# A decoder layer on one core: the second FFN product turned round, W_down stationary and the activations moving in 512 columns

## The chip, the core and the metric

The kernel runs on one core of one Trainium2 chip. The time is device microseconds of one execution; a result is the median of several executions. The kernel before takes 132.09 us (three runs, 131.9 to 132.27).

## What is computed

A pre-norm decoder layer for 16 sequences of 64 tokens with 256 features (1024 tokens, float32), in three steps with a residual each. The reference, cut to what matters here:

```python
x = x + self_attention(layernorm(x))            # 16 heads, causal, ALiBi, biases
x = x + cross_readout(layernorm(x), ctx, mask)  # scores with ctx, softmax, readout of ctx
def ffn(inputs, up_kernel, up_bias, down_kernel, down_bias):
    q_up, s_up = quantize_to_mxfp4(up_kernel, 32)
    x = mxfp4_matmul(inputs, q_up, s_up, 32) + up_bias        # 256 -> 1024
    x = gelu(x)
    q_dn, s_dn = quantize_to_mxfp4(down_kernel, 32)
    return mxfp4_matmul(x, q_dn, s_dn, 32) + down_bias        # 1024 -> 256
x = x + ffn(layernorm(x), ...)
```

The weights of the FFN are quantised in the kernel, in blocks of 32 rows with a power of two as scale. The quantised values are exact in bfloat16 and in float32r.

## The kernel before

The 1024 tokens are eight tiles of 128 (`TILES`). Two halves of four tiles go through the first layer norm and the projections q, k and v; from there the self attention, the cross attention and the third layer norm run tile by tile. The FFN runs in four groups of two tiles (`GT`, 256 tokens) and, in each, over eight blocks of 128 hidden features (`FC`). A step i = 8g + f of it has five stages:

- `up` (TensorE, L1160): four matmuls of 256 columns in float16 with `w_up_q` stationary, two parts of the normalised activations, into bank 0 or 1 in turn.
- `gelu` (ScalarE, L778): bias and gelu from the bank to `h_sb`.
- `round` (GpSimd, L630): `h_hi`, the value rounded to float32r.
- `split` (VectorE, L982): `h_lo`, what the rounding left.
- `down` (TensorE, L1176): for both tiles and both parts one matmul of 256 columns. The activations (`h_hi`, `h_lo`, 128 hidden features by 128 tokens) are stationary, the weights `w_down_q` move. All 32 matmuls of a group add up in one bank, tokens on the partitions.

After the last step of a group `final` (VectorE, L989) adds the bank to `x_sb`, once for each tile, and `store` (SyncE, L581) writes the tile of 128 KB. The bias of the second product has been added to `x_sb` before, by `add_down` on GpSimd (L634), once for each tile after its third layer norm, as `add_bo` (L591) adds the bias of the output projection.

The layer norms: `stats` on VectorE (L810, L811), `rstd` on GpSimd (L599, L603, L607), `norm` on ScalarE (L660) or VectorE (L819), `turn` on TensorE (L1015, transposes), `turn_copy` on ScalarE (L669, L672). Other stages that the prediction names: the projections q and k (L1028, float32 matmuls of 512 columns), the cross attention's scores (L1110, two float32 matmuls of 128 columns, and L1112), its transpose of the probabilities (L1118), readout (L1123).

The order of the work is not written by hand. `stages()` lists every stage with its engine, a duration, what it waits for and its banks; `schedule()` walks this table as a list scheduler and returns one order, and every engine's program goes through that order and emits its own stages. Among the ready stages that could start within `PATIENCE` of the first, the one with the longest way to the end wins, and `URGENCY` and `DRIFT` add to this way by name. The durations only set the order; on the chip the engines wait for each other by semaphores, and each engine's queue is in order:

```python
limit = starts[first] + patience.get(engine, 0.06)
key = max((k for k in starts if table[k][0] == engine and starts[k] <= limit), key=lambda k: (way[k], k))
```

A bank is claimed before it is written: TensorE waits in `claim` until the reader of what was last in the bank is done.

## Time and profile before

| what | value |
|---|---|
| median of 3 runs | 132.09 us (131.9 to 132.27) |
| the profiled execution, its own time | 132.44 us |
| its span in the trace | 130.6 us |
| TensorE busy (PE) | 116.4 us, 89% |
| TensorE weight loads (PEld) | 87.8 us, 67% |
| VectorE busy (DVE) | 103.5 us, 79% |
| ScalarE busy (ACT) | 88.7 us, 68% |
| GpSimd busy (POOL) | 81.5 us, 62% |
| data moved | 10.69 MB, mean 82 GB/s |

The page is one execution, taken by the hardware profiler. The span runs from the first to the last instruction or transfer that it shows; the execution's own time is 1.8 us longer. Busy time counts an instruction from its start to its end, and matmuls overlap: where two matmuls of a queue start 0.12 us apart, each may last 0.28 us. So distances between starts tell what TensorE can do, and durations do not. A float32 matmul stands in the trace as two matmuls (two passes), a float32 transpose, a float16 and a float32r matmul as one.

### The profile page before, as it was taken

The page shows a single profiled execution, that of the slowest core. Times are in us where ns is not written, and L with a number is a line of the kernel's source. Part 1 is how long each engine was busy: PE and PEld are TensorE (multiplying, and loading weights), DVE is VectorE, ACT ScalarE, POOL GpSimd, SP SyncE. Part 2 cuts the span into 40 slices and gives each one's busy share as a digit, 9 for nine tenths or more (in the row PEclk, how much of TensorE's full clock was granted, in tenths as well). Part 3 has the DMA queues.
Part 4 walks back from the last instruction along what each step waited for, and adds up shares of the span by engine and source line. Part 5 has one row for each costly group of instructions (what it writes and reads, how often), then busy time and mean ns, then how long its engine had stood idle before and what let it go on. Part 6 is the DMA issues. An engine that isn't in the chain of part 4 may idle for free.

```text
span 130.6 us, 3224 instructions
## 1 busy us (share of the span) xinstructions
PE 116.4 (89%) x1072; PEld 87.8 (67%) x1072; DVE 103.5 (79%) x227; ACT 88.7 (68%) x190; POOL 81.5 (62%) x144
## 2 busy tenths in 40 slices
PE   0997999698999899999989996979989599999990
PEld 0996447265534786677767684758878389999980
DVE  5678794799999999899999998778743985685632
ACT  1224679776999987977757875687957877754520
POOL 7685700153999976638038898787764567894330
PEclk9999999999999999999999999999999999999999
DMA  4799906999500000000000000000000200020202
GB/s 119 206 364 374 354 16 260 365 356 373 119 3 3 0 5 0 5 0 0 5 0 0 0 8 0 0 0 3 5 0 0 79 1 5 0 80 0 85 3 80
DMA packets 8879, 10.69 MB, mean 82 GB/s; under 512 B 1664, under 2 KB 7936, under 8 KB 8736
## 3 DMA queue, kind: packets, MB, share of 16 engines
q1 hardware_dynamic: 7776, 9.64, 22.1%
q10 hardware_dynamic: 1088, 0.86, 2.0%
q8 instruction: 9, 0.15, 0.5%
q14 instruction: 6, 0.05, 0.1%
HBM read 9.45 MB, written 1.05 MB: 80 GB/s over the span
## 4 chain that ended last, share of the span: by engine, by line
PE 29%; DVE 26%; POOL 18%; issue 18%; ACT 6%; DVEq 1%; POOLq 0%; ACTq 0%
POOL h_hi L630 6%; PE bank L1028 5%; PE bank L1176 5%; PE bank L1160 5%; DVE s_sb L857 5%; POOL rstd L603 5%; DVE s_max L862 4%; POOL var_eps L599 3%; PE bank L1040 3%; POOL x_sb L634 2%; DVE stats L810 2%; PE bank L1067 2%; PE bank L1059 2%; PE bank L1015 2%; POOL s_sb L641 2%
## 5 line engine op out<-in xcount | busy, mean ns | idle before, releaser
L641 POOL TENSOR_TENSOR s_sb<-s_sb,s_max 128x512 f32<-128x512 f32 x16 | 18.6, 1165 | 18.4 <-DVE s_max L862 18.2
L982 DVE TENSOR_TENSOR h_lo<-h_sb,h_hi 128x256 fp32r<-128x256 f32 x32 | 15.1, 485 | 7.6 <-POOL h_hi L630 7.5
L1160 PE MATMUL bank<-xn_T,w_up_q 128*128 128x256 f16 x128 | 19.4, 274 | 1.4 <-ACT h_sb L778 1.4
L778 ACT ACTIVATE h_sb<-bank,bias_cols 128x256 f32<-128x256 f32 x32 | 15.0, 472 | 7.7 <-PE bank L1160 5.9
L1176 PE MATMUL bank<-w_down_q,h_hi 128*128 128x256 f32 x64 | 19.2, 324 | 0.2 <-DVE h_lo L982 0.2
L630 POOL CAST h_hi<-h_sb 128x256 fp32r<-128x256 f32 x32 | 13.9, 440 | 8.0 <-ACT h_sb L778 7.6
L660 ACT ACTIVATE xn<-x_sb,shift,rstd 128x256 f32<-128x256 f32 x20 | 12.0, 599 | 7.7 <-POOL shift L607 3.2
L1176 PE MATMUL bank<-w_down_q,h_lo 128*128 128x256 f32 x64 | 16.4, 280 | 0.0
L603 POOL TENSOR_TENSOR rstd<-var_eps,minus_half 128x1 f32<-128x1 f32 x24 | 14.9, 622 | 2.0
L1028 PE MATMUL bank<-xn_T,w_T 128*128 128x512 f32 x32 | 14.7, 601 | 0.8 <-ACT xn_T L672 0.8
L599 POOL TENSOR_SCALAR var_eps<-mean_var 128x1 f32<-128x1 f32 x24 | 7.3, 304 | 10.7 <-DVE mean_var L811 9.5
L1160 PEld LDWEIGHTS bank<-xn_T,w_up_q 128*128 128x128 bf16 x128 | 10.5, 97 | 4.2 <-issue 1.4
L1176 PEld LDWEIGHTS bank<-w_down_q,h_hi 128*128 128x128 f32 x64 | 12.1, 189 | 0.8 <-issue 0.4
L1176 PEld LDWEIGHTS bank<-w_down_q,h_lo 128*128 128x128 f32 x64 | 12.2, 190 | 0.1
L1081 PEld LDWEIGHTS bank<-v,p_T 128*64 128x64 f32 x256 | 8.8, 137 | 4.5 <-issue 4.5
L857 DVE TENSOR_TENSOR s_sb<-bank,alibi_sb 128x512 f32<-128x512 f32 x16 | 10.9, 684 | 0.9 <-PE bank L1059 0.9
L724 ACT ACTIVATE p_T<-bank 128x512 f32<-128x512 f32 x16 | 9.5, 594 | 3.0 <-PE bank L1067 2.1
L1015 PE MATMUL bank<-const,xn 128*128 128x128 f32 x48 | 10.0, 296 | 1.6 <-ACT xn L660 1.2
L862 DVE TENSOR_REDUCE s_max<-s_sb 128x8 f32<-128x512 f32 x16 | 10.8, 675 | 0.1
L591 POOL TENSOR_TENSOR x_sb<-x_sb,row_biases_all 128x256 f32<-128x256 f32 x8 | 10.7, 1364 | 0.0
L1028 PEld LDWEIGHTS bank<-xn_T,w_T 128*128 128x128 f32 x32 | 5.8, 190 | 7.1 <-issue 7.1
L1081 PE MATMUL bank<-v,p_T 128*64 128x34 f32 x256 | 10.5, 226 | 0.0
(89 smaller groups left out, 265.5 us busy)
## 6 DMA issues: line engine op xcount, KB each, us to landing
raw_T<-in_W_up_T_dram SPq DMA_DIRECT2D x1, 1024.0 KB, 9.2
raw<-in_W_up_dram SPq DMA_DIRECT2D x1, 1024.0 KB, 11.5
raw_T<-in_W_down_T_dram SPq DMA_DIRECT2D x1, 1024.0 KB, 5.0
raw<-in_W_down_dram SPq DMA_DIRECT2D x1, 1024.0 KB, 7.8
ctx_T<-in_ctx_by_feature_dram SPq DMA_DIRECT2D x1, 1024.0 KB, 10.1
ctx_sb<-in_ctx_dram SPq DMA_DIRECT2D x1, 1024.0 KB, 13.8
out_dram<-x_sb SPq DMA_DIRECT2D x8, 128.0 KB, 1.7
x_sb<-in_x_dram SPq DMA_DIRECT2D x4, 128.0 KB, 3.1
```

The lines of the kernel that those rows point to most:

```text
L603: pool.tensor_tensor(rstd[:, n, t:t + 1], var_eps[:, n, t:t + 1], minus_half[:, :], ALU.pow).then_inc(rstd_ready[n], 1)
L630: pool.tensor_copy(h_hi[:, i % H_RING, :], h_sb[:, i % GELU_RING, :]).then_inc(rounded, 1)
L641: pool.tensor_tensor(tile, tile, s_max[:, u % S_RING, :].unsqueeze(2).broadcast_to([P, HC, S]), ALU.subtract).then_inc(centred, 1)
L778: act.activation(h_sb[:, i % GELU_RING, :], bank[up_bank(i)][:, 0:GN], ACT.Gelu_apprx_tanh, bias=bias_cols[:, BUP + f:BUP + f + 1], scale= ...
L857: dve.tensor_tensor(s_sb[:, u % S_RING, :], bank[u % EC][:, :], alibi_sb[:, u % EC, :], ALU.add).then_inc(scores_added, 1)
L862: dve.tensor_reduce(s_max[:, u % S_RING, :], s_sb[:, u % S_RING, :].rearrange("p (h k) -> p h k", h=HC), AX_X, ALU.max).then_inc(max_ready, 1)
L982: dve.tensor_tensor(h_lo[:, i % H_RING, :], h_sb[:, i % GELU_RING, :], h_hi[:, i % H_RING, :].bitcast(F32), ALU.subtract).then_inc(split_r ...
L1015: last = pe.transpose(dst[:, c * P:(c + 1) * P], xn[:, ring[t % len(ring)], c * P:(c + 1) * P], ident)
L1028: last = pe.matmul(dst[:, :], w_T[:, m, i, c * P:(c + 1) * P], half_tokens(h, i), start=(i == 0), stop=(i == EC - 1))
L1081: last = pe.matmul(dst[b * S:(b + 1) * S, first:first + width], p_T[:, u % 2, g, b * S:(b + 1) * S], v2[:, 2 * t + b, c * 4 + g, :, :].rea ...
L1160: last = pe.matmul(dst[:, 0:GN], w_up_q[:, c, f * P:(f + 1) * P], xn_T16[:, g * GT:(g + 1) * GT, at16:at16 + P], start=(k == 0), stop=(k = ...
L1176: last = pe.matmul(dst, src[:, i % H_RING, t * P:(t + 1) * P], w_down_q[:, f, :], start=(f == 0 and part == 0 and t == 0), stop=(f == FC - ...
```

## The change

The second product is turned round. `h_hi` and `h_lo` become the two halves of one tile `h_parts`, so that 512 columns (256 tokens in two parts) move at once, and `w_down_q` is stationary. A `down` stage is then two matmuls, one for each half of the 256 output features, each into a bank of its own, so a group holds two banks (`DOWN_BANKS`). The bank holds features by tokens: the sum of the high part in columns 0 to 255, that of the low part in columns 256 to 511.

What `final` did in token order no longer fits, so:

- `residual` (TensorE, new, eight stages): for each tile two matmuls with x stationary and the identity moving, 128 columns each, which add x, turned, into the bank's high half.
- `low_sum` (ScalarE, new, eight stages): the low half with the bias by feature goes to `x_sb`, whose two tiles of the group are free then.
- `final` (VectorE, eight stages as before): the high half is added to that. `store` writes 128 features by 256 tokens, 128 KB, to an output laid out by features.
- `add_down` on GpSimd is gone, and the load of the two row biases becomes a load of one.

The durations of many stages in `stages()` are renewed, `URGENCY`, `DRIFT` and `PATIENCE` are replaced, and with them the order on every engine. The diff, cut to its core:

```diff
-        add("add_down", (t,), "pool", 0.7, [("norm", (LN3, t))])
...
-            add("down", (i,), "pe", 0.56, [("split", (i,)), ("q_out", (DOWN, 1))], banks, ("final", (tiles[-1],)))
+            add("down", (i,), "pe", 0.39, [("split", (i,)), ("q_out", (DOWN, 1))], banks, [("final", (g, c)) for c in range(EC)])
         for t in tiles:
-            add("final", (t,), "dve", 0.33, [("down", (FC * g + FC - 1,)), ("add_down", (t,))])
-            add("store", (t,), "sp", 1.0, [("final", (t,))])
+            add("residual", (t,), "pe", 0.24, [("x2", (t,)), ("down", (FC * g,))])
+        for c in range(EC):
+            add("low_sum", (g, c), "act", 0.4, [("down", (FC * g + FC - 1,))] + [("residual", (t,)) for t in tiles])
+            add("final", (g, c), "dve", 0.35, [("low_sum", (g, c))])
+            add("store", (g, c), "sp", 1.0, [("final", (g, c))])
...
-        for name, us in (("q_divide", 1.13), ("q_exponent", 0.6), ("q_step", 0.6), ("q_add", 1.13), ("q_round", 1.13),
+        for name, us in (("q_divide", 1.85), ("q_exponent", 0.6), ("q_step", 0.6), ("q_add", 1.13), ("q_round", 1.13),
...
 PATIENCE = {
-    "pool": 0.54, "act": 0.04, "dve": 0.0, "pe": 0.0,
+    "pool": 0.34, "dve": 0.18, "act": 0.14, "pe": 0.1,
 }
...
-        h_hi = sb("h_hi", [P, H_RING, GN], F32R)
-        h_lo = sb("h_lo", [P, H_RING, GN], F32R)
+        h_parts = sb("h_parts", [P, H_RING, 2, GN], F32R)
+        h_hi, h_lo = h_parts[:, :, 0, :], h_parts[:, :, 1, :]
...
+                if stage == "low_sum":
+                    g, c = at
+                    act.wait_ge(down_ready, FC * (g + 1))
+                    act.wait_ge(residual_turned, GT * (g + 1))
+                    act.activation(out_by_feature(g, c), bank[down_bank(g, c)][:, GN:2 * GN], ACT.Identity,
+                                   bias=bias_cols[:, B_DOWN + c:B_DOWN + c + 1]).then_inc(low_sum_ready, 1)
...
                 if stage == "final":
-                    t, = at
-                    g = t // GT
-                    dve.wait_ge(down_ready, FC * (g + 1))
-                    dve.wait_ge(b_down_added, t + 1)
-                    dve.tensor_tensor(x_sb[:, t, :], bank[down_bank(g)][:, (t % GT) * E:(t % GT + 1) * E],
-                                      x_sb[:, t, :], ALU.add).then_inc(final_ready, 1)
+                    g, c = at
+                    dve.wait_ge(low_sum_ready, EC * g + c + 1)
+                    dve.tensor_tensor(out_by_feature(g, c), bank[down_bank(g, c)][:, 0:GN], out_by_feature(g, c),
+                                      ALU.add).then_inc(final_ready, 1)
...
-                    if f == 0:
-                        claim(down_bank(g), (final_ready, GT * (g + 1)))
-                    for t in range(GT):
-                        dst = bank[down_bank(g)][:, t * E:(t + 1) * E]
-                        for part, src in enumerate((h_hi, h_lo)):
-
-                            last = pe.matmul(dst, src[:, i % H_RING, t * P:(t + 1) * P], w_down_q[:, f, :],
-                                             start=(f == 0 and part == 0 and t == 0),
-                                             stop=(f == FC - 1 and part == 1), skip_group_check=True)
+                    for c in range(EC):
+                        if f == 0:
+                            claim(down_bank(g, c), (final_ready, EC * g + c + 1))
+                        last = pe.matmul(bank[down_bank(g, c)][:, :], w_down_q[:, f, c * P:(c + 1) * P],
+                                         h_parts[:, i % H_RING, :, :].rearrange("p s n -> p (s n)"),
+                                         start=(f == 0), stop=(f == FC - 1), skip_group_check=True)
                     last.then_inc(down_ready, 1)
+                if stage == "residual":
+                    t, = at
+                    g = t // GT
+                    pe.wait_ge(x2_ready, t + 1)
+                    first = t % GT * P
+                    for c in range(EC):
+                        last = pe.matmul(bank[down_bank(g, c)][:, first:first + P], x_sb[:, t, c * P:(c + 1) * P],
+                                         ident, start=False, stop=False, skip_group_check=True)
+                    last.then_inc(residual_turned, 1)
...
-DOWN_BANKS = (2, 3, 2, 3)
+DOWN_BANKS = ((2, 3), (4, 2), (3, 4), (5, 7))
```

How the order moves, at three places. The rows are instructions of one engine in program order, output before the arrow, operands behind it; numbers at names are banks.

TensorE, the end of the program. Before, the last up stage (into bank 1) is followed by four down stages and nothing else; the first of them and the beginning of the next:

```order
L1160 MATMUL bank1<-xn_T,w_up_q 128x256 x4
L1176 MATMUL bank3<-w_down_q,h_hi 128x256
L1176 MATMUL bank3<-w_down_q,h_lo 128x256
L1176 MATMUL bank3<-w_down_q,h_hi 128x256
L1176 MATMUL bank3<-w_down_q,h_lo 128x256
```

With the change, from the same up stage on, to the last matmul:

```order
L1166 MATMUL bank1<-xn_T,w_up_q 128x256 x4
L1179 MATMUL bank5<-h_parts,w_down_q 128x512
L1179 MATMUL bank7<-h_parts,w_down_q 128x512
L1189 MATMUL bank5<-const,x_sb 128x128
L1189 MATMUL bank7<-const,x_sb 128x128
L1179 MATMUL bank5<-h_parts,w_down_q 128x512
L1179 MATMUL bank7<-h_parts,w_down_q 128x512
L1189 MATMUL bank5<-const,x_sb 128x128
L1189 MATMUL bank7<-const,x_sb 128x128
L1179 MATMUL bank5<-h_parts,w_down_q 128x512
L1179 MATMUL bank7<-h_parts,w_down_q 128x512
```

The residuals of tiles 6 and 7 now stand between the last four down stages (L1179), of which the fourth ends the program.

TensorE, the end of the second group with the change (its banks are 4 and 2). L1129 is the cross attention's readout of the last tile, L1166 the up stages of steps 19, 20 and 21:

```order
L1129 MATMUL bank5<-ctx_sb,xp_T 128x256
L1179 MATMUL bank4<-h_parts,w_down_q 128x512
L1179 MATMUL bank2<-h_parts,w_down_q 128x512
L1179 MATMUL bank4<-h_parts,w_down_q 128x512
L1179 MATMUL bank2<-h_parts,w_down_q 128x512
L1166 MATMUL bank1<-xn_T,w_up_q 128x256 x4
L1166 MATMUL bank0<-xn_T,w_up_q 128x256 x4
L1166 MATMUL bank1<-xn_T,w_up_q 128x256 x4
L1179 MATMUL bank3<-h_parts,w_down_q 128x512
L1179 MATMUL bank4<-h_parts,w_down_q 128x512
```

Before, up and down stages take turns here, step by step. Now the eight down stages of the group stand with one up stage among them, and three up stages follow the last.

ScalarE, the same place with the change. L779 is gelu, L786 `low_sum`, L740 the exponential of the cross attention, L749 the copy of its probabilities:

```order
L740 ACT_TABLE_LOAD
L740 ACTIVATE xs_sb,xs_sum<-bank7,xs_negmax 128x128
L749 ACTIVATE xp_T<-bank6,valid 128x128
L740 ACTIVATE xs_sb,xs_sum<-bank7,xs_negmax 128x128
L749 ACTIVATE xp_T<-bank6,valid 128x128
L779 ACT_TABLE_LOAD
L779 ACTIVATE h_sb<-bank1,bias_cols 128x256
L786 ACTIVATE x_sb<-bank4,bias_cols 128x256
L779 ACTIVATE h_sb<-bank0,bias_cols 128x256
L786 ACTIVATE x_sb<-bank2,bias_cols 128x256
L779 ACTIVATE h_sb<-bank1,bias_cols 128x256
L661 ACTIVATE xn<-x_sb,shift,rstd 128x256
```

Before, ScalarE's gelus (L778) there have only normalisations and copies of the layer norm between them:

```order
L778 ACTIVATE h_sb<-bank0,bias_cols 128x256
L669 ACTIVATE xn_T<-bank6 128x256
L778 ACTIVATE h_sb<-bank1,bias_cols 128x256
```

So the gelu that frees bank 0 now stands behind the first copy, which waits for the last down stage of the group.

## Rows read from the trace of the kernel before

**Rows 1.** The page's section 1: busy us, share of the span, instructions.
```profile
PE 116.4 (89%) x1072; PEld 87.8 (67%) x1072; DVE 103.5 (79%) x227; ACT 88.7 (68%) x190; POOL 81.5 (62%) x144
```

**Rows 2.** Busy time in stretches: from:to, length, each engine's us and count, granted clock.
```profile
30.00:80.00 50.00, 48.41 (x528) 33.97 (x527) 48.31 (x93) 41.01 (x88) 36.32 (x45) 1.00 0.10 29
80.00:90.00 10.00, 7.78 (x80) 5.98 (x78) 7.72 (x18) 7.19 (x17) 7.90 (x13) 1.00 0.00 1
...
104.00:117.00 13.00, 12.63 (x107) 11.46 (x108) 9.59 (x23) 9.00 (x22) 10.53 (x24) 1.00 0.10 32
117.00:126.00 9.00, 9.00 (x80) 8.29 (x80) 5.22 (x13) 4.68 (x10) 4.28 (x11) 1.00 0.10 32
```

**Rows 3.** Timeline of TensorE: start us, us, what [idle before <-releaser].
```profile
81.68 0.44 PE L1015 MATMUL bank<-const,xn 128*128 128x128 f32 x2 [1.23 <-ACT xn L660]
...
103.66 0.30 PE L1118 MATMUL bank<-const,xs_sb 128*128 128x128 f32 x1 [0.92 <-DVE xn_T L825]
104.36 0.60 PE L1160 MATMUL bank<-xn_T,w_up_q 128*128 128x256 f16 x4 [0.40 <-ACT h_sb L778]
```

**Rows 4.** TensorE: one steady step in the timeline; source views of up and down.
```profile
110.39 0.61 PE L1160 MATMUL bank<-xn_T,w_up_q 128*128 128x256 f16 x4
110.75 0.37 PE L1176 MATMUL bank<-w_down_q,h_hi 128*128 128x256 f32 x1
110.96 0.28 PE L1176 MATMUL bank<-w_down_q,h_lo 128*128 128x256 f32 x1
...
111.19 0.28 PE L1176 MATMUL bank<-w_down_q,h_lo 128*128 128x256 f32 x1
111.32 0.61 PE L1160 MATMUL bank<-xn_T,w_up_q 128*128 128x256 f16 x4
...
L1160 PE MATMUL bank<-xn_T,w_up_q x36: 272/273/283, 117.2 to 124.9; 128*128 128x256 f16 x36
...
L1176 PE MATMUL bank<-w_down_q,h_hi x64: 278/287/470, 89.6 to 127.1; 128*128 128x256 f32 x64
```

**Rows 5.** Timeline of the weight loads of the same down stage.
```profile
110.84 0.19 PEld L1176 LDWEIGHTS bank<-w_down_q,h_lo 128*128 128x128 f32 x1
110.96 0.19 PEld L1176 LDWEIGHTS bank<-w_down_q,h_hi 128*128 128x128 f32 x1
```

**Rows 6.** Chain that ended last: the projections q and k, start us, us.
```profile
12.85 7.10 PE bank L1028 x16
```

**Rows 7.** Timeline of TensorE: a pair of transposes, the cross attention's scores.
```profile
98.57 0.38 PE L1015 MATMUL bank<-const,xn 128*128 128x128 f32 x2
99.81 0.62 PE L1110 MATMUL bank<-ctx_T,xn_T 128*128 128x128 f32 x4
```

**Rows 8.** Timeline of all engines at the end of the program.
```profile
124.60 0.61 PE L1160 MATMUL bank<-xn_T,w_up_q 128*128 128x256 f16 x4
126.83 0.35 PE L1176 MATMUL bank<-w_down_q,h_hi 128*128 128x256 f32 x1 [0.20 <-DVE h_lo L982]
127.27 0.28 PE L1176 MATMUL bank<-w_down_q,h_lo 128*128 128x256 f32 x1
127.58 0.76 DVE L989 TENSOR_TENSOR x_sb<-bank,x_sb 128x256 f32<-128x256 f32 x2 [0.90 <-PE bank L1176]
```

**Rows 9.** GpSimd's bias additions: their group, and pieces of the chain.
```profile
L634 POOL TENSOR_TENSOR x_sb<-x_sb,row_biases_all 128x256 f32<-128x256 f32 x8 | 5.8, 726 | 2.8 <-ACT xn L660 2.8
...
78.26 0.68 POOL x_sb L634
84.31 0.72 POOL x_sb L634
113.09 0.68 POOL x_sb L634
```

**Rows 10.** ScalarE: a copy of 256 columns from a bank; a gelu.
```profile
L672 ACT ACTIVATE xn_T<-bank 128x256 f32<-128x256 f32 x16 | 6.0, 378 | 4.6 <-PE bank L1015 4.6
...
104.37 0.47 ACT L778 ACTIVATE h_sb<-bank,bias_cols 128x256 f32<-128x256 f32 x1
```

107 lines of the change are left out of this document (52 added, 55 removed).

## The prediction

> **What bounds the kernel now.** I read the page's busy line first: TensorE is busy for 116.4 of 130.6 us, VectorE for 103.5, ScalarE for 88.7, GpSimd for 81.5 [rows 1]. That is an average, so the table by stretches comes next [rows 2]. From 30 to 80 us TensorE and VectorE are both about 97% busy. From 80 to 90 us TensorE falls to 7.78 of 10 us. From 104 us on it is busy almost without a break, and from 117 to 126 us for 9.00 of 9.00 us, at a granted clock of 1.00, its 2.4 GHz level, while VectorE needs 5.22 and ScalarE 4.68 us of the nine. So in the last quarter, where the change lies, TensorE's own work is the time, and a saved microsecond there is a saved microsecond. Third, TensorE's waits: after the start there are few, and the long ones lie between 80 and 105 us: 1.23 us for a normalised tile from ScalarE, 0.92 and 0.40 us around one of ScalarE's table loads [rows 3].
>
> **The down matmuls.** In the steady stretch one step is four up matmuls and four down matmuls, each of 256 columns. The up stages of two neighbouring steps start at 110.39 and 111.32 [rows 4]; over eight steps the source view gives 117.2 to 124.9 for first and last up matmul, less the 0.34 us by which the fourth starts after the first, so (7.7 - 0.34) / 8 = 0.92 us. Eight matmuls share it: 0.115 us each. At 2.4 GHz 256 columns take 0.107 us, if a column takes a cycle, which the up matmuls bear out: four in 0.61 us, less the 0.27 us of the last one, are 0.112 us apart. The change streams the same 2048 columns in six matmuls instead of eight. What can be gained is therefore only what lies between 0.117 us (the distance of the down matmuls) and 0.107 us, per matmul saved. No row shows a one-pass matmul of float32r with 512 columns. The bounds: 0.235 us, twice the present one, so no gain; and 0.213 us, columns alone. The nearest row is the float32 matmul of 512 columns, which the trace shows as two passes; 16 of them take 7.10 us [rows 6], 0.444 us each for 1024 cycles, so 0.222 us for 512. I take that: a down stage falls from 4 x 0.117 = 0.468 to 0.444 us, and 32 of them give back **0.8 us** (bounds 0 and 1.3).
>
> The 64 weight loads that go lie beside the matmuls: a load lasts 190 ns, yet the loads start 0.12 us apart, as the matmuls do [rows 4, 5]. So I count nothing more for them.
> The Trainium skill's page TensorE: Matmul & The Clock Gate (Back-to-back issue gap) gives a warm matmul N / 2.4 GHz plus 2.5 ns; by that rule, as an estimate, a down stage would save 2 x 2.5 ns and the whole change 0.2 us in place of the 0.8. The measured distance of the down matmuls, 0.117 us, is larger than the rule's 0.109, so the trace goes with the larger saving.
>
> **The residual by TensorE.** New are eight stages of two float32 matmuls with 128 columns, 16 matmuls in all, which turn x and add it into the bank. They are plain matmuls, not transposes. The cross attention's scores are that form: four passes for two matmuls, in 0.62 us less the last one's 0.28, so 0.113 us apart [rows 7]. With a little for the change of form around them, two matmuls cost 4 x 0.115 = 0.46 us, eight stages **3.7 us**. Below, a pair of transposes (0.38 us less 0.28, so about 0.1 us apart, one pass each) would make it 0.22 us a stage, 1.8 us in all. The nearest row is the scores', same type and same columns, so 3.7 us stand. On the path: tiles 2 to 5 wholly, 1.84 us; tiles 0 and 1 come while TensorE still has waits, I count half, 0.46 us; tiles 6 and 7 stand between the last down stages. There the old kernel has a hole: the last up stage starts at 124.60, its fourth matmul at 124.94, and the last down stage only at 126.83 because it waits for gelu, rounding and split [rows 8]. Between are three down stages, 1.40 us, so some 0.5 us are free (1.89 - 1.40, hardly less with the shorter stages), and of the 0.92 us 0.4 remain. Sum on the path **+2.7 us**.
>
> **The end.** Now two VectorE additions of 0.41 us follow the last matmul, from 127.58 to 128.34 [rows 8]. Afterwards ScalarE first evacuates the lower half with the bias. The row for such a copy is 378 ns [rows 10]; add a handover of 0.05 us, which the step from 127.55 to 127.58 and others bound. The second addition waits for the second copy, which starts some 0.3 us after the first: first copy to 0.41, first addition to 0.84, second to 1.25 us, against 0.76 now: **+0.5 us**. The stores are eight of 128 KB before and after.
>
> **GpSimd.** Eight additions of 726 ns leave, 5.8 us. Most ran where GpSimd had room. On the chain of waits pieces of them stand at 78.26 and 84.31, 0.68 and 0.72 us, just where TensorE is short of work and ScalarE waits for GpSimd's statistics; those at 113.09 and later lie under a full TensorE [rows 9]. **-1.4 us**; bounds 0 (the cover is VectorE, late next in that stretch) and -2.1.
>
> **ScalarE.** It gets eight copies, 3.0 us, in a stretch where it is about half busy, so no price for the time they take. But its queue is in order. Behind the first copy of the second group stands the gelu that frees bank 0 for the second of three up stages; both wait for the last down stage of the group. After that stage ends: 0.16 us until its result is there (0.28 less 0.117 [rows 8]), 0.05, copy 0.3 to 0.38, gelu 0.47 [rows 10], 0.05; about 1.05 us, of which the one up stage that can run covers 0.45. The next up stage stands behind another copy and gelu, 0.75 us, less 0.45. Together **+1.1 us** with a remainder for the normalisation between the next gelus. In the first and third group an up stage and another down stage cover the copy, and I count nothing. Against it, the new order fills the two holes of 0.92 and 0.40 us [rows 3] with a row of down stages, **-1.3 us**.
>
> Renewed durations and urgencies move many stages before 80 us too; there both big engines are full [rows 2], and none of their work goes, so nothing is counted. The bias load only becomes smaller. At the start GpSimd clears the mask before its first statistics instead of between them, the same work in another place; nothing.
>
> **Sum:** -0.8 + 2.7 + 0.5 - 1.4 + 1.1 - 1.3 = +0.8 us. The profiled execution took 132.44 us with a span of 130.6; its own would become 133.2. It stood 0.35 us above the median of three, 132.09, so I forecast 132.9 us. A measurement can tell about 0.3% from no change, 0.4 us, so "same" is 131.7 to 132.5.
>
> **The rivals.**
> *Cheap residual (faster).* The identity streams like in a transpose, 0.22 us a stage: on the path 0.46 x 2 for tiles 2 to 5, 0.23 for 0 and 1, nothing for 6 and 7, so 1.15 in place of 2.7; and the wide matmul takes 0.217 us, a saving of 1.1. The sum is then -1.05: 131.0 us, and 129.9 us if the hold on ScalarE does not come either. For it: TensorE's waits between 80 and 90 us are large. Against it: the scores' rows. Chance 0.30.
> *Weight loads were not hidden (faster).* If all that the steady step has above its columns, 0.92 - 0.853 = 0.07 us, came from four exposed loads and left with the change, 32 steps would give 2.2 us in place of 0.8: 131.5 us. Rows 5 speak against it: the loads overlap each other. Chance 0.05.
> The page named above (The mechanism, under packing) says that a weight load overlaps running matmuls only in other row groups, which all these loads share; by its load time of 128 / 1.2 GHz, 107 ns, an estimate would be 6.8 us less for 64 loads. The trace disagrees: eight loads and 2048 columns together take 0.92 us.
> *It cancels out (same).* Residuals fill waits to the last, or GpSimd's relief is worth 2.1 us: 132.1 us. Chance 0.15.
> *ScalarE is held in every group (slower still).* If in the first and third group too the copy reaches the head of the queue before the last down stage is done, two more holds of 1.1 us: 135.1 us; one of them gives 134.0. It decides from the point where the gelu ahead of the copy ends before that down stage. Chance 0.11.
> *The wide matmul is no cheaper (slower).* 0.235 us each, so the change does not do what it says: 133.7 us. Chance 0.05.
>
> **Numbers.** Forecast, slower by about 0.8 us, own range 132.5 to 134.3: 0.34. Slower in all 0.34 + 0.11 + 0.05 = 0.50, faster 0.35, same 0.15. The range from 129.9 to 135.0 us leaves out part of the cheap residual and the far end of the holds.
>
> **What would show it.** Down matmuls 0.22 us apart, steady step 0.89 to 0.90 us. Residual matmuls in passes 0.11 to 0.12 us apart, four to a stage. After the last matmul 1.25 us to the end of the last addition. One wait of TensorE for ScalarE of half a microsecond or more behind the eighth down stage of the second group. GpSimd's busy time 5.8 us less. The forecast is wrong if a residual stage takes 0.25 us, if the wide matmuls come less than 0.213 us apart, or if the time before the first down stage, now at 89.6 us [rows 4], changes by more than the work moved across it.

## The result, and the profile after

| | before | changed |
|---|---|---|
| median | 132.18 us (131.9 to 132.86, 4 runs) | **135.56 us** (134.79 to 136.28, 4 runs) |
| the profiled execution, its span | 132.44 us, 130.6 us | 136.28 us, 133.9 us |

The changed kernel is slower: ratio 1.026, 95% interval 1.021 to 1.031, that is 3.4 us in place of the 0.8 us forecast, and above the range (up to 135.0 us). The profiled execution stands 0.7 us above its median. Executions over 1.5% above the fastest of the same kernel are left out of its median and ratio; that touches one execution of the kernel before and one kernel below, whose trace is of such an execution.

The busy line of the page, and its chain by engine (before, the chain had 29% on TensorE):

```profile
PE 119.8 (89%) x1040; PEld 84.8 (63%) x1040; DVE 102.0 (76%) x227; ACT 90.6 (68%) x198; POOL 73.8 (55%) x136
...
PE 72%; ACT 8%; DVE 7%; issue 6%; POOL 2%; DMA 2%; ACTq 0%; DVEq 0%
```

The stretches, to be read against [rows 2]:

```profile
30.00:80.00 50.00, 49.03 (x518) 33.82 (x519) 47.96 (x94) 42.54 (x93) 34.67 (x46) 1.00 0.14 46
80.00:90.00 10.00, 7.82 (x83) 5.97 (x84) 8.42 (x24) 6.05 (x19) 4.75 (x9) 1.00 0.00 1
...
104.00:117.00 13.00, 12.30 (x75) 8.86 (x74) 8.21 (x23) 9.90 (x22) 5.93 (x16) 1.00 0.12 42
117.00:126.00 9.00, 9.00 (x60) 6.46 (x60) 5.31 (x14) 5.17 (x12) 3.67 (x8) 1.00 0.05 18
```

TensorE is busy 3.4 us longer and waits about as much as before. From 80 to 90 us GpSimd's work fell from 7.90 to 4.75 us, yet TensorE is no fuller than it was (7.82 against 7.78). From 104 to 117 us ScalarE is fuller than before, 9.90 us against 9.00. The granted clock is 1.00 in all of these.

Timeline of TensorE in the steady stretch and at the end of the program, and the two other engines behind it:

```profile
120.27 0.60 PE L1166 MATMUL bank<-xn_T,w_up_q 128*128 128x256 f16 x4
120.62 0.72 PE L1179 MATMUL bank<-h_parts,w_down_q 128*128 128x512 f32 x2
...
126.74 0.61 PE L1166 MATMUL bank<-xn_T,w_up_q 128*128 128x256 f16 x4
...
127.66 0.61 PE L1189 MATMUL bank<-const,x_sb 128*128 128x128 f32 x4
...
128.93 1.17 PE L1179 MATMUL bank<-h_parts,w_down_q 128*128 128x512 f32 x4
130.14 0.84 ACT L786 ACTIVATE x_sb<-bank,bias_cols 128x256 f32<-128x256 f32 x2 [2.23 <-PE bank L1179]
130.65 0.79 DVE L995 TENSOR_TENSOR x_sb<-bank,x_sb 128x256 f32<-128x256 f32 x2 [1.81 <-ACT x_sb L786]
```

Seven steps lie between the up stages at 120.27 and 126.74: 0.924 us each. Before it was 0.92 [rows 4], so the wide matmuls give nothing back. A residual stage shows as four passes in 0.61 us, less the last one's 0.28 as in [rows 7]: 0.11 us apart, about 0.45 us a stage. From the end of the last matmul, 130.10, to the end of the last addition, 131.44, it is 1.34 us, against 0.79 before (127.55 to 128.34 [rows 8]). To the end of the span it is 3.8 us against 3.1, so another 0.2 us lies in the last store.

TensorE's waits up to the first down stage, which starts at 93.93 us (before at 89.63 [rows 4]); of the 4.3 us between, some 2.65 are work that the new order has moved ahead of it (one output projection, one pair of the cross attention's scores, two of its transposes and readouts, two turns, less an up stage). This is an estimate from the distances between starts; at the smallest distances it is 2.5 us:

```profile
23.83 1.09 PE L1065 MATMUL bank<-k,q_T 64*64 64x256 f32 x16 [0.65 <-ACT q_T L680]
...
88.28 0.41 PE L1021 MATMUL bank<-const,xn 128*128 128x128 f32 x2 [1.18 <-ACT xp_T L749]
...
89.87 1.10 PE L1105 MATMUL bank<-w_T,q_T 128*128 128x256 f32 x4 [0.75 <-DVE x_sb L915]
...
91.38 0.60 PE L1166 MATMUL bank<-xn_T,w_up_q 128*128 128x256 f16 x4 [0.30 <-ACT h_sb L779]
```

The end of the second group, first TensorE and then ScalarE:

```profile
112.23 1.28 PE L1179 MATMUL bank<-h_parts,w_down_q 128*128 128x512 f32 x4
113.76 0.60 PE L1166 MATMUL bank<-xn_T,w_up_q 128*128 128x256 f16 x4 [0.25 <-ACT h_sb L779]
114.52 1.33 PE L1166 MATMUL bank<-xn_T,w_up_q 128*128 128x256 f16 x8 [0.17 <-ACT h_sb L779]
115.61 0.71 PE L1179 MATMUL bank<-h_parts,w_down_q 128*128 128x512 f32 x2
```

```profile
111.84 1.28 ACT L779 ACT_TABLE_LOAD   x1
113.14 0.47 ACT L779 ACTIVATE h_sb<-bank,bias_cols 128x256 f32<-128x256 f32 x1
113.54 0.47 ACT L786 ACTIVATE x_sb<-bank,bias_cols 128x256 f32<-128x256 f32 x1
113.91 0.47 ACT L779 ACTIVATE h_sb<-bank,bias_cols 128x256 f32<-128x256 f32 x1
```

From 112.23 to 115.61 TensorE has work for 4 x 0.235 + 12 x 0.1125 = 2.29 us in 3.38 us: a hole of 1.1 us, though each wait that the timeline shows is small. The old holes at 103.66 and 104.36 [rows 3] are gone.

Three marks of TensorE's timeline cut every run into the same stretches: its first projection v, the first scores of the self attention, and the first down stage. TensorE's first matmul and the first two marks in the kernel before, and in the changed one:

```profile
3.40 3.35 PE L1008 MATMUL bank<-const 128*128 128x128 f32 x14 [3.40 <-DMA const<-in_ident_heads_dram]
...
9.55 1.97 PE L1040 MATMUL bank<-w_T,xn_T 128*64 128x128 f32 x32
...
22.54 1.09 PE L1059 MATMUL bank<-k,q_T 64*64 64x256 f32 x16
```

```profile
3.91 3.35 PE L1014 MATMUL bank<-const 128*128 128x128 f32 x14 [3.91 <-DMA const<-in_ident_heads_dram]
...
10.02 1.97 PE L1046 MATMUL bank<-w_T,xn_T 128*64 128x128 f32 x32
```

The table has the stretches between them, in us of each profiled execution. It shows what the medians can't: apart from the start, a stretch that an edit doesn't touch comes out the same within 0.1 or 0.2 us, unless the granted clock falls in it. "Both" is float16 with the old front, or with the additions later; the last three rows are the mixed orders.

| kernel | start to v | v to scores | scores to first down | first down to the end of the span |
|---|---|---|---|---|
| before | 9.55 | 12.99 | 67.09 | 40.97 |
| changed | 10.02 | 13.81 | 70.10 | 39.97 |
| changed, no residual | 9.16 | 13.81 | 70.11 | 37.42 |
| changed, narrow | 9.40 | 13.82 | 70.10 | 40.08 |
| changed, float16 | 8.80 | 13.82 | 69.45 | 38.53 |
| changed, no hold | 8.47 | 13.81 | 70.65 | 40.17 |
| changed, old front | 9.32 | 12.99 | 70.42 | 39.87 |
| changed, additions back | 9.11 | 13.81 | 72.63 | 40.75 |
| changed, both | 9.02 | 12.98 | 69.75 | 38.55 |
| before, float16 | 9.09 | 12.99 | 66.17 | 39.95 |
| before, no additions | 9.75 | 12.99 | 65.25 | 40.91 |
| before, additions later | 8.79 | 13.00 | 65.24 | 41.07 |
| before, both | 9.32 | 12.99 | 65.32 | 39.97 |
| before, new front | 9.45 | 13.81 | 68.47 | 40.97 |
| new form, old tables | 8.75 | 12.99 | 69.26 | 48.70 |
| old form, new tables | 9.90 | 13.81 | 78.44 | 40.85 |
| changed, old order to the first up stage | 8.33 | 12.99 | 78.77 | 39.91 |

### The profile page after: what moved, and what is told of

It is laid out like the page before. It is cut to its first block, busy times and chain, and to the rows that moved or that the text cites. A ratio compares the mean times of both kernels' runs of the same rounds, so it can differ in the third digit from the quotient of the medians.

```text
span 133.9 us, 3159 instructions
## 1 busy us (share of the span) xinstructions
PE 119.8 (89%) x1040; PEld 84.8 (63%) x1040; DVE 102.0 (76%) x227; ACT 90.6 (68%) x198; POOL 73.8 (55%) x136
## 3 DMA queue, kind: packets, MB, share of 16 engines
HBM read 9.32 MB, written 1.05 MB: 77 GB/s over the span
## 4 chain that ended last, share of the span: by engine, by line
PE 72%; ACT 8%; DVE 7%; issue 6%; POOL 2%; DMA 2%; ACTq 0%; DVEq 0%
PE bank L1166 11%; PE bank L1179 10%; PE bank L1034 8%; PE bank L1087 6%; PE bank L1065 5%; PE bank L1021 4%; PE bank L1073 4%; PE bank L1105 4%; PE bank L1014 3%; PE bank L1046 3%; PE bank L1116 3%; PE bank L1189 3%; PE bank L1129 3%; DMA const<-in_ident_heads_dram 2%; POOL rstd L609 1%
## 5 line engine op out<-in xcount | busy, mean ns | idle before, releaser
L1179 PE MATMUL bank<-h_parts,w_down_q 128*128 128x512 f32 x64 | 22.4, 438 | 0.0
L636 POOL CAST h_parts<-h_sb 128x256 fp32r<-128x256 f32 x32 | 14.3, 462 | 13.3 <-ACT h_sb L779 8.1
L990 DVE TENSOR_TENSOR h_parts<-h_sb,h_parts 128x256 fp32r<-128x256 f32 x32 | 14.4, 471 | 9.3 <-POOL h_parts L636 9.3
L779 ACT ACTIVATE h_sb<-bank,bias_cols 128x256 f32<-128x256 f32 x32 | 15.0, 474 | 8.0 <-PE bank L1166 7.6
L1166 PE MATMUL bank<-xn_T,w_up_q 128*128 128x256 f16 x128 | 19.2, 274 | 1.0 <-ACT h_sb L779 0.7
L1166 PEld LDWEIGHTS bank<-xn_T,w_up_q 128*128 128x128 bf16 x128 | 10.6, 97 | 8.4 <-issue 7.3
L609 POOL TENSOR_TENSOR rstd<-var_eps,minus_half 128x1 f32<-128x1 f32 x24 | 14.0, 585 | 2.0
L673 ACT ACTIVATE xn_T<-bank 128x256 f32<-128x256 f32 x16 | 6.0, 379 | 6.8 <-PE bank L1021 6.7
L1179 PEld LDWEIGHTS bank<-h_parts,w_down_q 128*128 128x128 f32 x64 | 10.0, 191 | 0.7 <-issue 0.2
L718 ACT ACTIVATE s_sb<-s_sb 128x512 f32<-128x512 f32 x16 | 10.1, 629 | 0.4 <-POOL s_sb L642 0.4
L818 DVE BATCH_NORM_STATS2 stats<-x_sb 128x6 f32<-128x256 f32 x24 | 10.1, 419 | 0.3
L1105 PE MATMUL bank<-w_T,q_T 128*128 128x256 f32 x32 | 8.9, 400 | 0.9 <-DVE x_sb L915 0.7
```

Source lines behind the costliest of these rows:

```text
L609: pool.tensor_tensor(rstd[:, n, t:t + 1], var_eps[:, n, t:t + 1], minus_half[:, :], ALU.pow).then_inc(rstd_ready[n], 1)
L636: pool.tensor_copy(h_hi[:, i % H_RING, :], h_sb[:, i % GELU_RING, :]).then_inc(rounded, 1)
L779: act.activation(h_sb[:, i % GELU_RING, :], bank[up_bank(i)][:, 0:GN], ACT.Gelu_apprx_tanh, bias=bias_cols[:, BUP + f:BUP + f + 1], scale= ...
L990: dve.tensor_tensor(h_lo[:, i % H_RING, :], h_sb[:, i % GELU_RING, :], h_hi[:, i % H_RING, :].bitcast(F32), ALU.subtract).then_inc(split_r ...
L1105: last = pe.matmul(dst[:, 0:E], attn_T[:, c, t * P:(t + 1) * P], w_T[:, WO, c, :], start=(c == 0), stop=(c == EC - 1))
L1166: last = pe.matmul(dst[:, 0:GN], w_up_q[:, c, f * P:(f + 1) * P], xn_T16[:, g * GT:(g + 1) * GT, at16:at16 + P], start=(k == 0), stop=(k = ...
```

## The experiments

Every ratio is against the kernel before on the same chip, with its 95% interval. The stretches are those of the table.

**The two halves of the change.** One kernel has the new form with the old tables, the other the old form with the new tables and durations.

```diff
 URGENCY = {
-    "v": 296, "k": 202, "quant": 142, "q_divide": 80, ...
+    "quant": 142, "scores": 84, "attn_turn": 84, "k": 68, ...
```

> The new down form with its residual, low_sum and final, but with the urgencies, patience and durations of before (down 0.56 us). Theory A (the added TensorE work is the cost: the wide matmul gives nothing back, the residual adds 3.6 us, the end 0.5 us): as slow as the changed kernel, 135 to 135.8 us. Theory B (the new order is the cost: first scores 1.3 us later, first down stage 4.3 us later): 132.5 to 133.5 us.

> The old form (activations stationary, add_down on GpSimd), ordered with the changed kernel's urgencies, patience and renewed durations. Theory A: within 0.5 us of before, 132.2 us. Theory B: 134 us or more.

Measured: 140.92 us, 1.067 (1.059 to 1.074), and 145.15 us, 1.098 (1.092 to 1.104). Both are far slower than either parent, so they don't split the 3.4 us, and neither theory holds. Each form loses in the other's order: the first kernel behind the first down stage, 48.7 us against 40.0, the second ahead of it, 78.4 against 70.1. TensorE in the first of the two behind that stage, with a window (busy PE, PEld, DVE, ACT, POOL, then the granted clock):

```profile
114.67 0.44 PE L1021 MATMUL bank<-const,xn 128*128 128x128 f32 x2 [1.42 <-ACT xn L661]
117.46 1.86 PE L1166 MATMUL bank<-xn_T,w_up_q 128*128 128x256 f16 x8 [2.35 <-ACT h_sb L779]
...
116.00:120.00 4.00, 2.54 (x11) 1.59 (x11) 1.36 (x3) 2.62 (x5) 1.22 (x4) 0.55 0.00 1
```

Behind waits of 1.42 and 2.35 us eight up matmuls take 1.86 us, and the granted clock is 0.55, near the 1.2 GHz level. At a granted clock of 1.00 the changed kernel has eight in 1.08:

```profile
104.92 1.08 PE L1166 MATMUL bank<-xn_T,w_up_q 128*128 128x256 f16 x8
```

From 120 to 124 us the clock is 0.60. Together that is 4 x 0.45 + 4 x 0.40 = 3.4 us at most, about as much as the two waits: here a wait is paid twice.

**No residual by TensorE.** The output then lacks x in its last sum.

```diff
-                if stage == "residual":
-                    ...
-                        last = pe.matmul(bank[down_bank(g, c)][:, first:first + P], x_sb[:, t, c * P:(c + 1) * P],
-                                         ident, start=False, stop=False, skip_group_check=True)
-                    last.then_inc(residual_turned, 1)
```

> The changed kernel without the residual stages' 16 matmuls and the wait for them; x is then missing in the output's last sum. Theory A: 2.7 to 3.6 us faster than the changed kernel, 132 to 132.9 us. Theory B, where most of them hide in TensorE's waits: at most 1.2 us faster, 134.4 us or more.

Measured: 132.91 us, 1.005 (1.003 to 1.008). The residual costs 2.65 us of the 3.4, in the trace 2.55 us, all behind the first down stage (39.97 less 37.42). Theory A missed it by little: 2.7 us was its lower end.

**The down matmuls narrow again.** Each matmul of 512 columns is cut in two of 256 with the same stationary weights, so there are again 128 of them, with their loads.

```diff
+                        for part in range(2):
+                            last = pe.matmul(bank[down_bank(g, c)][:, part * GN:(part + 1) * GN],
+                                             w_down_q[:, f, c * P:(c + 1) * P], h_parts[:, i % H_RING, part, :],
```

> The changed kernel with each matmul of 512 columns cut into two of 256 for the same stationary block, same order. If a float32r column costs 1.1 cycles whatever the width: same time as the changed kernel within 0.3 us, down matmuls 0.117 us apart. If the changed kernel's wide matmul saves a fixed part of each matmul, and it is lost elsewhere: 0.8 us slower. If every weight load is held: more than 1 us slower.

Measured: 135.29 us, 1.023 (1.019 to 1.027), the changed kernel's time. Its steady step, where a stage is four matmuls:

```profile
120.67 0.61 PE L1166 MATMUL bank<-xn_T,w_up_q 128*128 128x256 f16 x4
121.04 0.72 PE L1180 MATMUL bank<-h_parts,w_down_q 128*128 128x256 f32 x4
121.60 0.61 PE L1166 MATMUL bank<-xn_T,w_up_q 128*128 128x256 f16 x4
```

0.93 us again. Neither the width nor the 64 loads are worth anything here.

**The second product in float16.** The same edit in the changed kernel and in the one before: activations in float16, weights in bfloat16 (their quantised values are exact in it).

```diff
-    w_down_q = sb("w_down_q", [P, FC, E], F32R)
-    h_parts = sb("h_parts", [P, H_RING, 2, GN], F32R)
+    w_down_q = sb("w_down_q", [P, FC, E], BF16)
+    h_parts = sb("h_parts", [P, H_RING, 2, GN], F16)
```

> The changed kernel with both parts of the activations in float16 and W_down in bfloat16, same order, same 512 columns. If the float32r column is what costs 1.1 cycles: the wide matmuls come 0.215 to 0.22 us apart, a steady step 0.88 to 0.89 us instead of 0.925, 1.0 to 1.4 us faster than the changed kernel, 134.2 to 134.6 us. If the step is held by anything else than TensorE's columns: no change, 135.3 to 135.6 us.

> The kernel before, its order and its down matmuls of 256 columns unchanged; only the number format of the second product is changed: h_hi and h_lo in float16 in place of float32r, w_down_q in bfloat16. Theory A (a float32r column costs about 1.1 cycles, a float16 column 1.04, whatever the width): the steady step falls from 0.925 to 0.87 to 0.88 us, 32 steps give at most 1.8 us; since part of the steps lies beside TensorE's waits I expect 0.8 to 1.5 us less than before, ratio 0.989 to 0.994. Theory B (the gain of the same edit in the changed kernel came from the waits around its down stages and not from the columns): steady step still 0.92, time within 0.4 us of before.

Measured: 133.46 us, 1.011 (1.005 to 1.017), 2.0 us less than the changed kernel and more than the 1.0 to 1.4 expected; and 129.99 us, 0.984 (0.981 to 0.988), 2.0 us less than before. TensorE in the first, then in the second:

```profile
117.55 0.60 PE L1166 MATMUL bank<-xn_T,w_up_q 128*128 128x256 f16 x4
117.98 0.59 PE L1179 MATMUL bank<-h_parts,w_down_q 128*128 128x512 f16 x2
118.42 0.60 PE L1166 MATMUL bank<-xn_T,w_up_q 128*128 128x256 f16 x4
```

```profile
115.31 0.60 PE L1160 MATMUL bank<-xn_T,w_up_q 128*128 128x256 f16 x4
115.75 0.27 PE L1176 MATMUL bank<-w_down_q,h_hi 128*128 128x256 bf16 x1
...
116.19 0.60 PE L1160 MATMUL bank<-xn_T,w_up_q 128*128 128x256 f16 x4
```

The step is 0.87 to 0.88 us with wide and with narrow matmuls, so 0.05 us shorter than in float32r; 32 of them would be 1.7 us. Behind the first down stage the changed kernel gains 1.44 of it, the one before, which has holes there, 1.02. What the step had above its columns belongs to the number format. Ahead of the first down stage float16 gives 0.65 and 0.92 us more, by shorter waits: the one for gelu before an early up stage, 0.71 us before, is 0.23 us in the second kernel. No down matmul runs there, so these are not TensorE's columns. What got shorter is VectorE's writing of the quantised weights, which is narrower too. In the changed kernel, and in its float16 copy with TensorE's wait behind it:

```profile
85.86 1.21 DVE L980 TENSOR_TENSOR w_down_q<-q_x,q_scale 128x1024 fp32r<-128x1024 bf16 x1
```

```profile
84.66 0.67 DVE L980 TENSOR_TENSOR w_down_q<-q_x,q_scale 128x1024 bf16<-128x1024 bf16 x1
...
86.55 0.41 PE L1021 MATMUL bank<-const,xn 128*128 128x128 f32 x2 [0.64 <-ACT xp_T L749]
```

The write is 0.54 us shorter, and so is that wait, 0.64 us in place of 1.18. It stands in VectorE's queue ahead of the maximum of the cross attention's scores, on which the copy of the probabilities depends. So the edit changes two things, and of the gain of 2.0 us only the part behind the first down stage is TensorE's.

**GpSimd's additions left out of the kernel before.** The bias of the second product is missing.

```diff
-                if stage == "add_down":
-                    t, = at
-                    ...
-                    dve.wait_ge(b_down_added, t + 1)
```

> The kernel before without GpSimd's eight additions of the down bias (the bias is left out of the output), same order. If they were on the path as the prediction had it (-1.4 us): 130.7 us. If VectorE or the latency of the chain takes their place: 131.8 to 132.2 us.

Measured: 130.18 us, 0.986 (0.980 to 0.993), 1.85 us less, and in the trace 1.84 us between the first scores and the first down stage. TensorE's wait of 1.23 us at 81.68 [rows 3] is gone. In the old order the relief is real, and larger than the 1.4 us counted.

**The additions back in the changed kernel**, as eight idle additions of the same size.

```diff
+                if stage == "extra":
+                    t, = at
+                    pool.wait_ge(xn_ready[LN3], t + 1)
+                    pool.tensor_tensor(extra[:, t, :], bo_all[:, :], bo_all[:, :], ALU.add)
```

> The changed kernel in its own order, frozen, with eight idle additions of 128x256 put back on GpSimd, each behind the third layer norm of its tile (a wait for the normalised tile, then an addition into a buffer that nobody reads), one or two GpSimd stages behind that tile's statistics as add_down stood before. They price GpSimd's relief in the new order. Theory A (in the new order GpSimd waits 2.5, 1.8, 1.0 and 1.2 us for VectorE's statistics between 78 and 91 us, so the relief is worth nothing there): 135.2 to 136.0 us, ratio to before 1.023 to 1.029. Theory B (the relief is worth what leaving the additions out gave in the old order, 1.85 us): 137 to 137.5 us, ratio about 1.038.

Measured: 138.35 us, 1.048 (1.045 to 1.052), 2.8 us more than the changed kernel. Theory A, mine, fell, and B had too little. TensorE, and two windows of it alone (busy, granted clock):

```profile
81.28 0.33 PE L1302 MATMUL bank<-const,xs_sb 128*128 128x128 f32 x1 [1.61 <-ACT xs_sb L918]
...
80.00:84.00 4.00, 2.72 (x11) 0.72 0.00 0
84.00:88.00 4.00, 3.95 (x45) 0.86 0.00 0
```

Its long waits sum to 3.73 us (1.61, and 0.75, 0.86, 0.51 later), those of the changed kernel up to there and beyond to 2.47 (0.24, 1.18, 0.75, 0.30): 1.3 us more. The clock takes the rest: 4 x 0.28 + 4 x 0.14 = 1.7 us at most. Theory A's pauses of GpSimd are there, but no addition fell into them: three stand at 65.7, 70.6 and 77.1 us, the next at 93.9. The third stands straight ahead of GpSimd's subtraction of the row maxima for the self attention. Counted from the first scores, this ends at 56.8 us against 55.0 in the changed kernel, and ScalarE's exponential starts as much later. So a pause of GpSimd for VectorE says nothing about the room ahead of it. That this lateness makes the 1.61 us of TensorE is read from the trace, not tested.

**The additions later in the kernel before.** Nothing is left out; only GpSimd's queue is in another order. Of the frozen order, GpSimd's stages around the first of them:

```diff
     ('rstd', (2, 0)), ('centre', (12,)),
-    ('add_down', (0,)),
     ('rstd', (1, 3)), ('centre', (13,)),
     ...
     ('round', (7,)), ('rstd', (2, 3)),
+    ('add_down', (0,)),
     ('rstd', (1, 7)),
+    ('add_down', (1,)),
```

> The kernel before, its order frozen, with GpSimd's eight bias additions moved later on GpSimd's queue: those of tiles 0 to 4 into the pauses between 94 and 104 us, those of tiles 5 to 7 between the roundings of steps 18 to 23. Nothing is left out. Theory A (the additions cost only by their place, before the statistics that TensorE waits for at 81.7 us): most of the 1.85 us that leaving them out gave comes back, 130.3 to 131.0 us, ratio 0.987 to 0.993. Theory B (GpSimd's load as such costs, at any place in that stretch): less than 0.5 us, ratio above 0.996.

Measured: 130.21 us, 0.987 (0.983 to 0.991), 1.8 us less than before, close to Theory A. The stretch to the first down stage is 65.24 us, as without them (65.25): all that they cost was their place. Of TensorE's waits between 80 us and the first down stage only this one is left:

```profile
84.28 0.60 PE L1329 MATMUL bank<-xn_T,w_up_q 128*128 128x256 f16 x4 [0.71 <-ACT h_sb L947]
```

**No hold at the end of the second group.** The changed kernel, its two low sums of that group moved behind the gelu of step 20, the two last additions behind that step's split, and the banks so that nobody waits for them.

```diff
-DOWN_BANKS = ((2, 3), (4, 2), (3, 4), (5, 7))
+DOWN_BANKS = ((2, 3), (4, 2), (3, 5), (7, 4))
...
-    order = schedule()
+    order = ORDER
```

> The changed kernel with a fixed order in which the second group's two copies on ScalarE stand behind the gelu of step 20, their additions behind its split (and other banks for the third and fourth group). If the hold of some 1 us at the end of the second group is real: 0.7 to 1.1 us faster, 134.4 to 134.8 us, and no gap between the last down stage of the group and the up stages. If it only moves: within 0.3 us of the changed kernel.

Measured: 135.93 us, 1.032 (1.025 to 1.038), no gain. Ahead of the first down stage, where nothing was edited, this execution is 0.55 us longer at a granted clock of 0.58 from 88 to 92 us; behind it the stretch is 40.17 us against 39.97 and 40.08 in the changed kernel and its narrow twin, so there is no gain without that either. TensorE's waits there:

```profile
112.77 1.03 PE L1337 MATMUL bank<-xn_T,w_up_q 128*128 128x256 f16 x8 [0.25 <-ACT h_sb L950]
114.07 0.60 PE L1337 MATMUL bank<-xn_T,w_up_q 128*128 128x256 f16 x4 [0.27 <-ACT h_sb L950]
116.50 0.60 PE L1337 MATMUL bank<-xn_T,w_up_q 128*128 128x256 f16 x4 [0.22 <-ACT h_sb L950]
```

The waits moved to later gelus. So the copies held nothing by standing in front. What the traces of both kernels show in their place is a full queue of ScalarE: a table load of 1.28 us stands at the head of its row of gelus and copies, and no pause follows it in the changed kernel up to 116.8 us. No run moved the table load, so that it is the cause is not tested.

**The old front.** The changed kernel with the order of the kernel before up to the first scores; and the kernel before with the new front.

```diff
-    order = schedule()
+    order = ORDER
```

> The changed kernel with the order of before up to the first scores stage, the rest as changed. The first scores come 0.7 us later in the new order. If that delay lasts to the end: 134.6 to 134.9 us. If the full VectorE behind it absorbs it: 135.3 to 135.6 us.

> The kernel before with the changed kernel's order up to the first scores and its own order behind it, frozen. Theory A (the front of the new order makes the first scores later and this lasts to the end): 132.8 to 133.1 us, ratio 1.006 to 1.009. Theory B (it costs only together with the rest of the new order): within 0.3 us of before, ratio 0.998 to 1.002.

Measured: 134.54 us, 1.019 (1.014 to 1.025), 1.0 us less than the changed kernel. The stretch from v to the first scores is 12.99 us again instead of 13.81; 0.3 us is given back behind it (70.42 against 70.10), so by the stretches 0.6 us of it last to the end. The work ahead of those scores is the same in both orders, in another sequence; what is new is the wait of 0.65 us for ScalarE's copy of q, the result that the scores need last.

And 135.23 us, 1.025 (1.020 to 1.031), 3.0 us more than before on the same chip, far over the 0.8 expected. Granted clock 0.65 in this stretch of it:

```profile
28.00:32.00 4.00, 4.00 (x41) 2.99 (x35) 3.96 (x8) 1.50 (x3) 1.93 (x3) 0.65 1.03 361
```

The front costs 0.82 us in both kernels, to the hundredth. Here it costs 1.38 us more up to the first down stage: the clock loses 4 x 0.35 = 1.4 us at most from 28 to 32 us. In the changed kernel it keeps its 1.00 there.

**The old order up to the first up stage**, in the changed kernel.

> The changed kernel with the order of the kernel before (without the eight GpSimd additions) up to its first up stage, that is to about 85 us, and the changed order for what is left; the order is frozen. Theory A (the three waits of 1.18, 0.75 and 0.30 us before the first down stage belong to the new order of the stretch from 80 to 91 us, in which the old order, relieved of the additions, would have only 0.7 us): they shrink to about 1 us in all, 1.2 us less than with the old front alone, 133.2 to 133.6 us, ratio about 1.010. Theory B (the seam between two orders or the changed form brings waits of its own): 134.3 us or more, ratio above 1.017, as with the old front alone or worse.

Measured: 140.48 us, 1.063 (1.056 to 1.070); the trace is of an execution of 142.41 us. It leaves the question open, since the clock takes most of the difference. TensorE, and two windows with all engines:

```profile
82.16 0.44 PE L1192 MATMUL bank<-const,xn 128*128 128x128 f32 x2 [1.76 <-ACT xn L832]
83.62 0.30 PE L1295 MATMUL bank<-const,xs_sb 128*128 128x128 f32 x1 [1.02 <-DVE xn_T L1004]
...
84.00:88.00 4.00, 3.15 (x17) 2.19 (x19) 1.84 (x7) 2.20 (x6) 2.12 (x6) 0.59 0.00 0
88.00:92.00 4.00, 4.00 (x36) 3.15 (x33) 2.22 (x5) 1.22 (x4) 0.00 (x0) 0.50 0.01 2
```

There are waits of 1.76 and 1.02 us, and the clock then stood at 0.50 to 0.63 for 12 us, 5.1 us at most; from 24 to 32 us it lost up to 1.7 more (0.83 and 0.74). That is most of the 8.35 us by which this stretch is longer than with the old front alone. Behind the first down stage nothing is lost (39.91 us).

**Both edits of each kernel together.** The changed kernel with float16 and the old front; the kernel before with float16 and the additions later. The edits are those shown.

> The changed kernel with both edits that helped it alone: the second product's activations in float16 and its weights in bfloat16 (2.0 us less by itself), and the order of the kernel before up to the first scores, the rest of the order as changed (1.0 us less by itself). Theory A (the two lie in different stretches and add up): 132.3 to 132.8 us, about level with before, ratio 1.002 to 1.006. Theory B (the later front is hidden by the same waits that the shorter down stages shorten): 133.2 to 133.6 us, ratio about 1.010.

> The kernel before with both edits that helped it alone: GpSimd's additions moved later (1.8 us less by itself) and the second product in float16 and bfloat16 (2.0 us less by itself). Theory A (waits before the first down stage and columns behind it are separate terms): 128.1 to 128.6 us, ratio 0.970 to 0.975, the fastest kernel of this study. Theory B (float16 gained by shortening the same waits): 129.2 us or more, ratio above 0.979.

Measured: 132.59 us, 1.005 (1.001 to 1.008), both gains nearly in full (2.0 and 1.0), as Theory A has it; and **129.33 us**, 0.978 (0.974 to 0.981), the fastest kernel here, 2.9 us below the one before. Of the 3.8 us of its two parts 0.9 is missing; the time is in Theory B's range. The table says where: behind the first down stage float16 gives its 1.1 us, but ahead of it, where it gave 0.92 by itself, the stretch stays at 65.32 us. There the wait for gelu, which float16 alone had cut to 0.23 us, is 0.71 us again.

## Why the prediction was wrong

The direction was right, the size was not. The table of stretches takes the sum apart; 2.65 us of work moved across the first down stage are taken out of both sides (with 2.5 us the two rows would shift by 0.15 us against each other):

| stretch | counted | found |
|---|---|---|
| start to v | 0 | +0.47 |
| v to the first scores | 0 | +0.82 |
| scores to the first down stage | -1.4 (relief) | 70.10 - 67.09 - 2.65 = +0.36 |
| behind it | -0.8 + 2.7 + 0.5 + 1.1 - 1.3 = +2.2 | 39.97 - 40.97 + 2.65 = +1.65 |
| sum | +0.8 | +3.3 |

The 0.47 us of the start is chance. In these two traces it is the first load's: TensorE's first matmul waits for it until 3.40 us before and 3.91 us in the changed kernel, and from there to v it is 6.15 and 6.11 us. In kernels with the changed kernel's order up to there the load lands between 3.30 and 3.91 us. The miss of 2.5 us is made by two steps ahead of the first down stage, 0.82 and 1.76 us; that the last stretch came out 0.55 better and the start 0.47 worse nearly cancels.

**"Nothing is counted" before 80 us** is the step that failed most plainly: 0.82 us in place of 0. It rests on [rows 2], but that row begins at 30 us, and the loss lies ahead of it: the first scores came at 23.83 us, behind a wait of 0.65 us for ScalarE's copy of q. The kernel with the old front has the 0.82 us back, and 0.6 of them last to the end. That neither engine's work changes says nothing about when it can begin.

**GpSimd's relief** failed as a term of this sum, 0.36 in place of -1.4, and not as a mechanism. The additions cost 1.85 us in the old order and 2.8 in the new, up to 1.7 of that by the clock. But I took the old order's waits, let the additions go, and kept the rest. The new order has waits of its own there, 1.18, 0.75 and 0.30 us, of the same total as the old 1.23, 0.71 and 0.29: for the probabilities' copy, for x after the cross attention's readout (it frees the bank), and for gelu. I had named this only as a bound ("VectorE, late next"), and for the first it was: 0.54 of the 1.18 us hang on VectorE's write of the weights ahead of it, as float16 shows. What placements make the rest stays open: the mixed order that should have told it lost 5 us or more to the clock.

**The down matmuls** were mis-sized, 0 in place of -0.8. The step that failed is the "nearest row", and it was misread. The 16 in [rows 6] are rows of the trace, and a float32 matmul is two of them. The source view of that line in the kernel before:

```profile
L1028 PE MATMUL bank<-xn_T,w_T x32: 592/592/697, 12.9 to 41.7; 128*128 128x512 f32 x32
```

The eight stages q and k are 16 matmuls and show as 32 rows, so the 7.10 us are eight matmuls, and 0.444 us is one pass of 512 columns, not two. A pass takes twice the time of its columns at a cycle each, as the scores' 0.113 us for 128 columns does too. Half of it is a rate and no matmul of the trace: no row shows 512 columns in 0.222 us. The excess of 0.117 over 0.107 us was read as a cost per matmul. It goes with the columns, by number format. The upper bound, 0.235 us, was the truth; the rival that said so had 0.05 and deserved far more, since the up matmuls of the same width stand 0.112 us apart in the same rows: the count alone could not make the difference. The Trainium skill's page TensorE: Matmul & The Clock Gate (Back-to-back issue gap) was the better guide in size. By its rule 256 columns take 0.109 us and 512 take 0.216; the float16 kernels agree, with 0.11 and 0.22. The float32r rows, 0.117, don't fit it, but the saving of the change by it, 0.2 us as an estimate, was nearer than mine.

**The residual** was right in mechanism and size, 2.65 us in place of 2.7 (2.55 in the trace): the scores' form was the right row, and the rival that it streams like a transpose is refuted. **The end** too, +0.55 in place of +0.5 up to the last addition; the 0.2 us in the last store were put at nothing.

**Hole and holes.** The rest behind the first down stage, the last store with it, is 1.65 - 2.55 - 0.55 = -1.45 us, where +1.1 and -1.3 and the -0.8 of the down matmuls stood. The old holes are gone as foreseen, and a third of 0.36 us at 96 us with them. The hole of the second group stands in the trace, but the copies' place before the gelus is not its cause: moving them bought nothing. The traces point to ScalarE's row behind a table load, which no run tested. So its 1.1 us is no price of the copies' place, and how much of it the old order would not have had is not separated. The rival of a hold in every group did not come.

## What to carry to other kernels

A change that renews the order has to be costed on the new order: walk it for the first use of each late result, above all before the stretch where the bounding engine is full, instead of taking the old waits away one by one. Cost a matmul by its number format and columns, and look for an engine's small works that only stand in a bad place: moving eight additions down a queue gave 1.3% and left nothing out. A change of number format changes the engines that write the operands as well. Mixing two tuned orders can measure the seam more than the part.

## What was not expected of the hardware

- A float32r matmul is dearer by column than a float16 one, with 256 and with 512 columns: the step of 2048 columns takes 0.924 us against 0.87, with 1024 of its columns changed.
- A pass of a float32 matmul takes 0.113 us for 128 columns and 0.444 for 512, and a matmul has two. A whole float16 matmul takes 0.112 us for 256 columns and 0.22 for 512.
- VectorE writes 128x1024 elements from bfloat16 in 1.21 us as float32r and in 0.67 us as bfloat16.
- 64 weight loads of 190 ns fewer changed nothing: the narrow twin, with its loads, takes 135.29 us against 135.56. The Trainium skill's page TensorE: Matmul & The Clock Gate (The mechanism, under packing) says that a load overlaps running matmuls only in other row groups, and beside it names a background weight buffer as the other way for a load to be pulled ahead. The loads here all share their row groups with the matmuls and start 0.12 us apart under running matmuls, so the trace and this run disagree with the first sentence by itself.
- At the start TensorE comes to full speed at a moment that differs between executions of the same work: three identity matmuls at 7 us (six passes) take 1.49 us in the kernel before and the changed one, 0.83 in the kernel with no hold. That is nearly the ratio of the clock's two levels, but the granted clock shows 1.00 for both, so the cause is inferred. With the landing of the first load, between 3.19 and 3.91 us, this puts the first projection between 8.3 and 10.0 us in the seventeen traces, one of each kernel, and moves the whole time by more than several of the edits are worth. Stretches between marks of the trace are free of it.
- The granted clock fell in several kernels, behind waits of TensorE that came close together: to 0.72 behind 1.61 us (additions back), to 0.59 and then 0.50 behind 1.76 and 1.02 us, to 0.55 behind 1.42 and 2.35 us, and to 0.65 behind 0.72, 0.41 and 0.67 us. The changed kernel has waits of 1.18, 0.75 and 0.30 us within 4 us and keeps its 1.00 in the execution shown; its copy with the low sums moved, with the same 1.18 and 0.75, fell to 0.58 behind them. So a wait can cost twice its length, and whether it does is not decided by the order alone.
